# A decoder layer on one core: the last 32 rows of the attention heads' latents through 64x64 quarters of TensorE's array instead of 64x128 halves

## What is computed

```python
q_hk = (hidden_q @ Wq.T).reshape(Bv, Sv, H, K)              # H = 16 heads, K = 128
q_big = jnp.einsum('bshk,hkq->bshq', q_hk, w_kc_q)          # 192 channels a head
q_big = _apply_rope(q_big, ...)
q_r = jnp.einsum('bshq,hqr->bhsr', q_big, W_qr)
k_r = jnp.einsum('bld,hdr->bhlr', kv_r, W_kr)               # kv_r: 64 channels
scores = jnp.einsum('bhsr,bhlr->bhsl', q_r, k_r)
attn = jax.nn.softmax(scores, axis=-1)
ctx_c = jnp.einsum('bhsl,bld->bhsd', attn, kv_r)
```

## Time and profile before

| | us |
|---|---|
| median of 3 runs | 531.21 |
| lowest and highest | 529.97, 535.25 |
| the profiled execution, its own time | 533.35 |
| its span, from the first to the last instruction | 531.5 |

### The profile page before, as it was taken

The page is one execution under the profiler, slowest core; times in us unless marked ns, Lnnn a source line. Parts: engine busy times, 40 slices in busy tenths (PEclk is TensorE's granted clock), DMA queues, the critical chain, the costliest instruction groups (busy, mean ns, idle before and its releaser), DMA issues.

```text
span 531.5 us, 10547 instructions
## 1 busy us (share of the span) xinstructions
PE 430.6 (81%) x3616; PEld 345.8 (65%) x3616; DVE 404.7 (76%) x742; ACT 311.5 (59%) x722; POOL 217.2 (41%) x157
## 2 busy tenths in 40 slices
PE   4979923838777586777999999999999999998733
PEld 1435623527667475666888888888888888887512
DVE  1967699978999969996575687877778777876453
ACT  3666996959999969985143444535255453525320
POOL 2300009985987949780323232323233232322010
PEclk9999975978899879967999999999999999999765
DMA  8942633053011511103000000000000000000000
GB/s 295 389 205 81 195 93 108 20 120 110 21 41 30 145 54 51 39 21 123 22 1 2 11 2 22 0 0 20 0 20 0 20 0 0 20 0 20 1 10 10
DMA packets 18652, 30.85 MB, mean 58 GB/s; under 512 B 2112, under 2 KB 11712, under 8 KB 17920
## 3 DMA queue, kind: packets, MB, share of 16 engines
q1 hardware_dynamic: 18624, 30.49, 17.4%
HBM read 24.16 MB, written 6.32 MB: 57 GB/s over the span
## 4 chain that ended last, share of the span: by engine, by line
PE 40%; issue 19%; DVE 19%; ACT 9%; POOL 8%; DMA 3%; SPq 1%; DVEq 1%; POOLq 0%; ACTq 0%
PE ps L410 33%; POOL reg_b L1059 5%; PE ps L532 3%; DVE reg_b L1256 3%; PE ps L629 2%; ACT hc L854 2%; DMA ud_t<-ud_dram 2%; POOL reg_b L1082 2%; DVE ps L1249 2%; DVE ps L1246 2%; DVE reg_b L1309 1%; ACT reg_b L944 1%; ACT ps L846 1%; DVE reg_b L1194 1%; POOL small L1064 1%
## 5 line engine op out<-in xcount | busy, mean ns | idle before, releaser
L1059 POOL TENSOR_TENSOR reg_b<-reg_c,reg_a 128x1024 f32<-128x1024 f32 x56 | 130.4, 2369 | 58.8 <-DVE reg_c L1199 58.6
L1082 POOL TENSOR_TENSOR reg_b<-reg_b 128x768 f32<-128x768 f32 x32 | 58.0, 1811 | 134.5 <-DVE reg_b L1309 107.3
L410 PE MATMUL ps<-x1T,Mw 128*128 (+1 forms) x768 | 95.2, 281 | 0.0
L410 PEld LDWEIGHTS ps<-x1T,Mw 128*128 128x128 f32 x768 | 89.9, 195 | 4.4 <-issue 3.9
L854 ACT ACTIVATE hc<-reg_b,bc 128x512 f32<-128x512 f32 x112 | 80.4, 718 | 20.9 <-PE ps L532 14.7
L532 PE MATMUL ps<-ident,hc 128*128 128x128 f32 x452 | 73.0, 309 | 19.7 <-ACT hc L854 19.3
L1256 DVE SCALAR_TENSOR_TENSOR reg_b<-reg_c,bc,ps 128x512 f32<-128x512 f32 x112 | 81.8, 736 | 0.0
L532 PEld LDWEIGHTS ps<-ident,hc 128*128 128x128 f32 x452 | 58.9, 160 | 30.5 <-ACT hc L854 29.3
L1249 DVE TENSOR_TENSOR ps<-ps,reg_b 128x512 f32<-128x512 f32 x96 | 65.7, 690 | 8.9 <-ACT ps L846 8.8
L846 ACT ACTIVATE ps<-reg_b 128x512 f32<-128x512 f32 x112 | 66.2, 592 | 4.1 <-POOL reg_b L1059 4.1
L944 ACT ACTIVATE reg_b<-ps,small 128x128 f32<-128x128 f32 x128 | 45.1, 367 | 24.5 <-DVE small L1314 24.5
(11 more groups left out here) (143 smaller groups left out, 709.9 us busy)
## 6 DMA issues: line engine op xcount, KB each, us to landing
reg_a<-a_dram SPq DMA_DIRECT2D x4, 1024.0 KB, 7.3
Mw<-w_o SPq DMA_DIRECT2D x1, 2048.0 KB, 15.3
ud_dram<-reg_b SPq DMA_DIRECT2D x4, 512.0 KB, 4.4
zs_dram<-x1T SPq DMA_DIRECT2D x4, 512.0 KB, 3.7
ud_t<-ud_dram SPq DMA_DIRECT2D x8, 256.0 KB, 3.1
zs_t<-zs_dram SPq DMA_DIRECT2D x8, 256.0 KB, 2.6
xw<-x_fm SPq DMA_DIRECT2D x2, 512.0 KB, 6.1
mring<-w_q SPq DMA_DIRECT2D x4, 256.0 KB, 4.1
```

Source lines behind the costliest of these rows:

```text
L410: return pe.matmul(o, l, r, start=start, stop=stop)
L1059: pool.tensor_tensor(dA[:, g % RING], delta_r[:, bass.ds(t, 1), :].to_broadcast([P, SA, DI]), Abc[:, g * SA:(g + 1) * SA, :], ALU.mult).th ...
L1082: pool.tensor_tensor(rq[:, g % 2].rearrange("p a c n -> p (a c n)"), pc[:, g % 2].rearrange("p a c n -> p (a c n)"), psn[:, g % 2].rearran ...
```

## The change

Both uses of the array by quarters now have one form. The four products of 64x128 for the rests of 32 become eight of 64x64: each column half of the same weight block is a product by itself. What is read, what is written and what is summed into PSUM stays the same; the increment for ScalarE is on the last of the eight.

```diff
                 for ab in range(2):
-                    for r in range(2):
-                        rows = slice(r * DC, (r + 1) * DC)
-                        last = mm(latent_of[:, r, :], Nw[rows, g, ab, P:2 * P], rq[rows, g % 2, ab, 2, :],
-                                  False, ab == 1)
+                    for c, r in ((0, 0), (1, 1), (1, 0), (0, 1)):
+                        rows, cols = slice(r * DC, (r + 1) * DC), slice(c * DC, (c + 1) * DC)
+                        last = mm(latent_of[cols, r, :], Nw[rows, g, ab, P + c * DC:P + (c + 1) * DC],
+                                  rq[rows, g % 2, ab, 2, :], False, ab == 1)
                 last.then_inc(qmm, 1)
```

## The result

The changed kernel takes 528.88 us (median of 20 runs, 526.44 to 532.48), the kernel before beside it 532.75 us (median of 20, 529.42 to 537.18 but for one run of 718.59). The ratio is 0.9926, 95% interval 0.9904 to 0.9947, so the change takes 2.8 to 5.1 us away. The forecast was 3.3 us less, and a span of 528.2 us for the profiled execution; it has 528.3.

A forecast was written before the change was run, and what follows sets the result against it. TensorE bounds the first two and last steps, VectorE's chain the steady steps; 1.66 + 1.03 + 0.62 = 3.3 us off the median 531.21 gives 527.9 us, range 524.8 to 531.2 (8 in 10).

The forecast's parts named there:

- The price of a call: Each to_latent call on TensorE falls from 1.24 us to 1.02 to 1.04, a saving taken as 0.207 us.
- the upper bound: If shared rows of rq serialised each wave of four quarters into two, a to_latent call would be 0.23 us longer.
- The first two steps: Start of the attention part: TensorE alone sets the pace, eight calls on the path, 1.66 us saved.
- VectorE itself hangs on scores and the FFN's product, which move up too: In the last of the first eight calls VectorE's slack is smaller, but its inputs come earlier, so all eight count.
- second rival: Less comes through: first eight calls give half, steady steps nothing; 1.4 us saved, 529.8 us; chance 0.15.
- The steady steps: Steps 2 to 6 close over VectorE; one to_latent of four is on the path, 5 x 0.207 = 1.03 us saved.
- The other three only lengthen TensorE's wait: In a steady step three of four to_latents save no time; TensorE's wait before L629 grows from 0.28 to about 0.9 us.
- The last step: Step 7: the path is TensorE's own from the handover on, three calls, 0.62 us saved; the 32nd call gives nothing.
- The sum: 1.66 + 1.03 + 0.62 = 3.3 us saved, 16 calls out of 32 counting; span from 531.5 to 528.2 us.
- The first (every call): Rival: all 32 to_latent calls count, 6.6 us saved, 524.6 us; chance 0.08.
- The third: Rival: the new quarters run two abreast, +0.23 us a call, 5.7 us slower in sum, 536.9 us; chance 0.05.
- fourth: Rival: TensorE idles longer before L629 and its clock falls to 0.50 in six steps; 12 us slower, 543; chance 0.01.

The follow-up runs named there:

- e4: Kernel before with the same 12 products ordered quarters, halves, quarters, halves; a call took 1.60 us instead of 1.24, the span 540.8 us (one execution).
- e1: Kernel before with the quarters only in the calls of head group 0, halves kept in groups 1 to 3; 530.07 us beside 531.15, steady steps 30.68 us.
- e7: Changed kernel with VectorE's row maxima of slot 3 ahead of the quantization in steps 2 to 6; 523.53 us (median of six), 0.9797 of the kernel before.
- e5: Changed kernel with the eight new products reordered, both parts of one quarter behind each other; 1.10 us a call, steady steps 30.63 us.

## Why the prediction was right, point by point

- **The price of a call.** Right: 1.04 us, a saving of 0.207. The new quarters run four abreast; the shared rows of rq, from which the upper bound was worked out, cost nothing that the rows show. It was right also that what goes is a switch and not work of the products: e4 put in two switches at the same products and paid 0.36 us for them.
- **The first two steps.** Eight calls on the path, 1.66 us, was 0.3 too much. From one execution to the other L629 of step 2 came 1.25 us earlier, or 1.34 against the first call, which lay 0.09 later (259.65 against 259.56). The step that failed is "VectorE itself hangs on scores and the FFN's product, which move up too": they moved up, but onto GpSimd's addition, which stretched VectorE's work. This is the mechanism of the second rival, at about a sixth of its price (0.3 us of the 1.9 that it would take from the 3.3).
- **The steady steps.** One call of four on the path was the right reading of the waits, and the page's chain, which gave TensorE the stretch, the wrong one. The failed step is "The other three only lengthen TensorE's wait": the second one counts by half, 0.11 us, since VectorE's chain touched TensorE once more. I had looked at brackets only. In steps 3 to 6 a step lost 0.31 us. Step 2 lost only 0.09, since it began in the kernel before with VectorE early (its L1366 took 1.06 us there) and now begins like the others.
- **The last step.** 0.63 us against 0.62 forecast, three calls; L629 of step 7 was 2.60 us earlier than before and the one of slot 3 in it 3.23. VectorE's wait in front of its maxima fell from 0.61 to 0.21.
- **The sum.** 1.34 + 0.09 + 4 x 0.31 + 0.63 = 3.3 us. The forecast's 1.66 + 1.03 + 0.62 is the same number from terms of which the first was 0.3 too high and the second 0.3 too low. It was right in the mechanism and in the price of a call, and lucky in that two terms of second order cancelled. Luck, too, is that the two profiled executions agree at the start of the attention part, ahead of the first call: from 250 to 252 us, with TensorE busy throughout, the granted clock is 0.50 (the 1.2 GHz level) in both, and 1.00 in e1. There the way from the first projection to the first L629, with two calls in it, takes 14.68 us, where it takes 16.53 in the kernel before and 16.13 in the changed one. Of the 1.85 us between e1 and the kernel before, one cheaper call makes 0.21. Single spans can differ by the rest without any change, so the 528.3 proves less than the lengths of the steps do.
- **Rivals.** The first (every call) is what happens once VectorE's chain is shortened, not in this kernel. The second shows at the start of step 2 alone. The third and fourth, the slower ones, are out: a call never took more than 1.04 us in the changed kernel, and the granted clock from 262 to 488 us is 1.00.

## What to carry to other kernels

Products of two shapes side by side cost a switch each way; giving the few odd ones the shape of their neighbours can pay even when it doubles their number, if the array takes as many abreast as there are more. How much of it reaches the time is decided elsewhere: count, per step of the schedule, which of the instances lie between a handover and the next wait of the saving engine, and look for handovers by the distances between instructions, since a wait of 0.1 us has no bracket. When an engine's wait grows after a change (here 0.28 to 0.80 us), that shows gain still to be had (e7 gave 1.10 us a step), and the other engine's chain is the thing to shorten next: one reordered reduction, worth 0.9% on the kernel before, turned the change's 0.7% into 2.0% for both together.

## What the runs showed of the hardware that was not expected

- Opening a shape has a price that depends on the shape: 0.21 us for 64x128 halves behind quarters (what the change saves a call), 0.15 us for 64x64 quarters behind halves (the rest of e4's 0.36).
- The order of products over the quarters hardly matters: 1.10 us for 32 instructions with two products of a quarter in sequence, 1.04 when all four alternate; instructions of different quarters start out of the order of the program (e5, four starts within 0.04 us).
- VectorE's operations between two parts of SBUF stretch beside GpSimd's addition: 0.64 in place of 0.29 us for the quantization's L1356, and 1.29, 1.06 or 0.57 us for the same L1366, the shorter the less of it lies beside the addition. Whenever it begins, the stretched operation ends a fixed time behind the addition: L1366 0.28 or 0.29 us (371.04 behind 370.76 in e7, 370.39 behind 370.10 in the changed kernel), L1356 0.15 (301.82 behind 301.67). That fits an operation that waits for the addition to end, and not one that runs at a lower pace.
